# ScalarE copies the three plain edge fields, GpSimd adds the second weight parts: a two-layer graph network on Trainium2

## The reference

```python
h = relu(layernorm(x))
x = x + segment_sum((h @ W0)[src] * edge_weight[:, None], dst)
h = relu(layernorm(x)) @ W1.T + b1            # einsum('nd,od->no')
deg = 1 + count of edges with row == n        # self loops added
x = x + segment_sum(deg[row]**-.5 * deg[col]**-.5 * h[col], row)
```

## Time and profile before

| what | value |
|---|---|
| three runs | 1748.29, 1748.61, 1752.34 us |
| profiled execution, own time | 1750.08 us |
| its span | 1748.3 us |
| granted TensorE clock, mean of the span | 0.966 |
| busy PE / DVE / ACT / POOL, share of the span | 89% / 53% / 26% / 32% |

### The profile page before, as it was taken

One profiled execution on the slowest core, in us unless ns is written; L12 is line 12 of the kernel. 1 busy time (PEld: TensorE's weight loads), 2 busy tenths in 40 slices (PEclk: granted clock), 3 DMA queues, 4 the chain that ended last, 5 costly groups with the idle time before them and its releaser, 6 DMA issues.

```text
span 1748.3 us, 30157 instructions
## 1 busy us (share of the span) xinstructions
PE 1554.0 (89%) x8627; PEld 792.7 (45%) x8628; DVE 930.2 (53%) x1747; ACT 456.5 (26%) x783; POOL 556.2 (32%) x1494
## 2 busy tenths in 40 slices
PE   2566699995979999999998999979999999999998
PEld 1233355543545454444554545334444444444443
DVE  6956556425977678777776776382313131313121
ACT  2514454531212222222222222271212121212110
POOL 0112444213656677677676774000000000000000
PEclk9977899997989999999999999999999999999999
DMA  7201242107546565666565666671232323232310
GB/s 262 97 1 32 64 139 61 29 16 165 114 97 141 125 142 135 144 145 139 133 151 129 146 140 150 201 230 55 63 99 66 96 66 96 66 96 66 96 37 25
DMA packets 449659, 185.86 MB, mean 106 GB/s; under 512 B 376677, under 2 KB 431993, under 8 KB 449544
## 3 DMA queue, kind: packets, MB, share of 16 engines
q1 hardware_dynamic: 449544, 184.63, 41.5%
HBM read 77.06 MB, written 77.11 MB: 88 GB/s over the span
## 4 chain that ended last, share of the span: by engine, by line
PE 54%; DVE 14%; issue 11%; POOLq 5%; POOL 5%; DMA 4%; SPq 4%; DVEq 2%; ACT 2%; ACTq 0%
PE pair L1392 19%; PE pair L1304 12%; PE pair L1253 9%; PE pair L1316 7%; PE pair L1265 5%; POOLq L522 3%; POOL fbuf L525 2%; SPq L357 2%; POOL fbuf L527 2%; DVE slots L774 2%; DMA a_scratch<-area 2%; DVE slots L775 2%; DVE h L939 1%; PE pair L1422 1%; SPq L378 1%
## 5 line engine op out<-in xcount | busy, mean ns | idle before, releaser
L1316 PE MATMUL pair<-h,area 128*128 128x512 f16 x2400 | 551.0, 383 | 2.6 <-issue 1.9
L1316 PEld LDWEIGHTS pair<-h,area 128*128 128x128 f16 x2400 | 234.2, 99 | 265.5 <-issue 18.2
L1265 PE MATMUL pair<-slots 128*128 128x240 f16 x1624 | 209.3, 275 | 104.8 <-DVE slots L775 54.6
L525 POOL CAST fbuf<-etab 128x12 f16 (+1 forms) x640 | 192.9, 301 | 152.4 <-DVE slots L775 79.2
L1048 ACT ACTIVATE area<-pair 128x320 f32<-128x320 f32 x160 | 69.9, 437 | 643.2 <-PE pair L1265 439.9
L1265 PEld LDWEIGHTS pair<-slots 128*128 128x128 f16 x1624 | 157.3, 100 | 171.4 <-issue 73.0
L979 DVE SCALAR_TENSOR_TENSOR agg_s<-pair,sc,agg_s 128x512 f16<-128x512 f32 x40 | 28.2, 747 | 350.7 <-ACT agg_s L1172 350.7
L1304 PE MATMUL pair<-wmat,agg_t 128*128 128x512 f16 x960 | 210.4, 379 | 1.6 <-ACT agg_t L1179 1.6
L527 POOL TENSOR_TENSOR fbuf<-etab,negbase 128x4 f16 (+2 forms) x640 | 200.9, 314 | 0.0
L1392 PE MATMUL pair<-h,etab 128*128 128x512 f16 x800 | 182.1, 379 | 8.9 <-DVE h L939 8.7
L1392 PE MATMUL pair<-h,slots 128*128 128x512 f16 x800 | 180.5, 379 | 0.0
(11 more groups left out here) (181 smaller groups left out, 1316.1 us busy)
## 6 DMA issues: line engine op xcount, KB each, us to landing
c_scratch<-area SPq DMA_DIRECT2D x160, 160.0 KB, 2.2
a_scratch<-area SPq DMA_DIRECT2D x320, 80.0 KB, 2.2
area<-c_scratch SPq DMA_DIRECT2D x20, 1280.0 KB, 7.3
xt<-in_x SPq DMA_DIRECT2D x19, 512.0 KB, 3.6
x_scratch<-xt SPq DMA_DIRECT2D x19, 512.0 KB, 2.9
xt<-x_scratch SPq DMA_DIRECT2D x19, 512.0 KB, 3.6
out_x<-xt SPq DMA_DIRECT2D x19, 512.0 KB, 2.6
h<-x_scratch SPq DMA_DIRECT2D x4, 2048.0 KB, 10.5
```

The lines of the kernel that those rows point to most:

```text
L525: pool.tensor_copy(fbuf[:, s, 1:F, at].rearrange("p f u d -> p u f d"), twice(etab_c[:, bass.ds(c, u), 1:F], [P, u, F - 1, 2])).then_inc(s ...
L1265: return pe.matmul(dest, touches[:, t, 0:P], touches[:, t, P:CS], start=first, stop=last, skip_group_check=True)
L1316: last = pe.matmul(sum_pair(e)[:, half * H:(half + 1) * H], wts(e)[:, q, k, :], hpart(k, r)[:, half * H:(half + 1) * H], start=k == q == r ...
```

## The change

It has four parts.

- The copy of the three plain fields leaves GpSimd and becomes a ScalarE activation (`ACT.Copy`), in a `fields` of ScalarE's own, with its own load of the chunk number. GpSimd keeps the load and the addition of the key. There are 640 copies in all, four per quad.
- ScalarE issues the copies for quad n+2 just ahead of `window_out(n)`. They wait for the one-hots that read the same half of `fbuf` before.
- The addition of the weights' second parts, L823, leaves VectorE. `sum_counts` on GpSimd now waits for `win_evac` (VectorE's L820) in place of `win_act` (ScalarE's L1050), does this addition first and signals `win_lo`, on which the stores wait, and then adds to the degrees. There are 160 such additions.
- One-hots wait on two semaphores, `step_keys` and `step_fields`. The last tile is taken out of ScalarE's loop, since the last two quads have no later fields.

```diff
@@ GpSimd
-                    pool.tensor_copy(fbuf[:, s, 1:F, at].rearrange("p f u d -> p u f d"),
-                                     twice(etab_c[:, bass.ds(c, u), 1:F], [P, u, F - 1, 2])).then_inc(step_fields, 1)
                     pool.tensor_tensor(fbuf[:, s, 0, at], twice(etab_c[:, bass.ds(c, u), 0], [P, u, 2]),
-                                       twice(negbase[:, bass.ds(v0 + w, 1)], [P, u, 2]), ALU.add).then_inc(step_fields, 1)
+                                       twice(negbase[:, bass.ds(v0 + w, 1)], [P, u, 2]), ALU.add).then_inc(step_keys, 1)
...
             def sum_counts(n, s):
-                pool.wait_ge(win_act, n + 1)
+                pool.wait_ge(win_evac, n + 1)
+                pool.tensor_tensor(a_stage(s)[:, 1], a_stage(s)[:, 1], a_stage(s)[:, 2], ALU.add).then_inc(win_lo, 1)
@@ VectorE
-                dve.wait_ge(step_fields, 2 * UP_STEPS(n))
+                dve.wait_ge(step_keys, UP_STEPS(n))
+                dve.wait_ge(step_fields, UP_STEPS(n))
...
-                dve.wait_ge(win_evac, n + 1)
-                nc.vector.tensor_tensor(a_stage(s)[:, 1], a_stage(s)[:, 1], a_stage(s)[:, 2], ALU.add).then_inc(win_lo, 1)
@@ ScalarE
+            def fields(n, s, v0, count, u):
+                need(act, hots_ready, n - 1)
+                for w in range(count):
+                    act.load(c_reg, wtab[0:1, bass.ds((v0 + w) * 4, 1)])
+                    c = act.snap(c_reg[0], min_val=0, max_val=NCH)
+                    act.activation(fbuf[:, s, 1:F, w * u:(w + 1) * u].rearrange("p f u d -> p u f d"),
+                                   twice(etab_c[:, bass.ds(c, u), 1:F], [P, u, F - 1, 2]),
+                                   ACT.Copy).then_inc(step_fields, 1)
...
             def tile(td):
                 for q in range(QPT):
                     n = QPT * (td + PRE) + q
+                    if isinstance(n, int) and n < UQ:
+                        fields_of(2 * n + 2, 0)
+                        fields_of(2 * n + 3, 1)
+                    elif not isinstance(n, int) or n + 2 < NQ:
+                        fields_of(n + UQ + 2, q % 2)
                     window_out(n, q % 2, 2 * n + 2 if isinstance(n, int) and n < UQ else n + UQ + 1)
```

More of the change, by code:

```diff
@@ L225, in gnn_two_layers @@
         sup_free = sem("sup_free")
+        step_keys = sem("step_keys")
         step_fields = sem("step_fields")
@@ L1050, in window_out, with fields_of @@
                 act.activation(a_stage(s)[:, 2], sums[:, :, 2 * SB:3 * SB], ACT.Copy, scale=A_DOWN).then_inc(win_act, 1)
+            c_reg = [act.alloc_register("act_chunk")]
+            def fields(n, s, v0, count, u):
[6 more added lines that the diff above has]
+                                   ACT.Copy).then_inc(step_fields, 1)
+            def fields_of(n, s):
+                if isinstance(n, int) and n < 2 * UQ:
+                    fields(n, s, 2 * n, 2, UP)
+                else:
+                    fields(n, s, 4 * n - 4 * UQ, 4, UL)
             def STORED(n, s):
@@ L1121, in _ @@
                     act.wait_ge(table_ready, 1)
+                    act.wait_ge(etab_ready, F)
+                    fields_of(0, 0)
+                    fields_of(1, 1)
                 if t == min(W1_AT):
@@ L1129, in _ @@
                         std({1: 3, 6: 4, 9: 5}[w])
+                    fields_of(2 * w + 2, 0)
+                    fields_of(2 * w + 3, 1)
                     window_out(w, w % 2, 2 * w + 2, True)
@@ L1134, in _ @@
                 tile(td)
-            with act.Fori(UQ // QPT - PRE, T - PRE) as td:
+            with act.Fori(UQ // QPT - PRE, T - PRE - 1) as td:
                 tile(td)
+            tile(T - PRE - 1)
             def counts_first(e, done):
```

## The result

The changed kernel takes 1778.31 us (median, 1774.99 to 1779.54); the kernel before took 1748.45 us on the same chip (1747.96 to 1752.34). The ratio is 1.016, 95% interval 1.014 to 1.018. The change costs 29.9 us; the prediction had 11.8 for it, so it had the sign and not the size.

What follows compares the result with a forecast made beforehand. TensorE was taken to bound 447 to 1090 us, idling 50 us there. Nine pairs (+9.4 us) and quads 16 to 31 (+2.4) summed to +11.8 us, so 1760 us as a median, range 1738 to 1790.

Steps and rivals of the forecast that it cites:

- the term of -0.56 us for VectorE's branch back: In tiles with VectorE's branch back, it starts earlier by L823, -0.56 us, taking most of the 0.74 us wait.
- VectorE, per quad: Without L823 one-hots are ready 0.52 us sooner; one GpSimd addition of 320 elements costs them 0.67 us.
- the chain with L823 at both ends: From the last quad's L823 via stores, transposes and the next tile's L823 to TensorE's late step: 19 us.
- The term of +0.75 us for a tile without the branch back: Late step behind the transposes comes later: +0.2 us at the chain's start, +0.55 us at its end.
- ScalarE's copies at no cost: 640 ScalarE copies at 0.53 us each, 2.1 us a quad; lateness hidden by TensorE's dense products, cost none.
- GpSimd: right: GpSimd's quad: four key steps of 0.53 us and two additions of 0.90, 3.9 us against TensorE's 4.06; it just fits.
- The collision's 0.67 us: On VectorE's one-hots, one GpSimd addition of 320 elements running among them delays them by 0.67 us.
- The first tile of a pair: The tile with VectorE's branch back: earlier branch, longer addition and later chain end together give +0.3 us.
- "Quads 16 to 31", +2.4 us: Quads with two steps each and little VectorE room: each saves 0.52 and pays 0.67 us, 16 x 0.15.
- The count, nine pairs: 18 tiles (quads 16 to 159) make 9 pairs, each 1.05 us slower: +9.4 us.
- The rival with VectorE's relief: VectorE's relief from L823 outweighs collisions, making the kernel faster: 1739 us, or 1726 if one-hots never pay; chance 0.22.
- GpSimd and ScalarE as the bound: Two rivals, 1785 us each: GpSimd at 4.5 us a quad, chance 0.10; ScalarE's copies late, chance 0.08.

## Why the prediction was right or wrong

Three steps of the prediction failed: the term of -0.56 us for VectorE's branch back, which measured +1.52 us; the term "VectorE, per quad", which counted one collision where two occur; and a term that is missing, what a longer wait does to TensorE's clock, which is half of the loss (14.2 of 25 us).

*What bounds the kernel, and the chain with L823 at both ends: right.* The late steps stayed at the places of the earlier trace rows. The term of +0.75 us for a tile without the branch back measured +0.87, and about +1.0 with the loop written out.

*ScalarE's copies at no cost: right in the step between them, wrong at the branch back.* They stand 0.52 to 0.53 us apart, as read from GpSimd's step. Alone they cost 0.3%, and nothing once both loops are written out. But "VectorE takes it up only after the one-hots of quad n+1, later than that" does not hold for the last quad ahead of the branch back: the subtraction waits for `window_out` there. Writing ScalarE's loop out gave the changed kernel 10 us back, and nothing to the kernel before with VectorE's loop written out. That the copies in ScalarE's loop make the difference fits this, but the two were not compared with all else the same.

*GpSimd: right.* The addition took 0.854 us for 0.86; the key step rose with it, to 0.401 us, and GpSimd did not become the bound. The collision's 0.67 us was met to a hundredth: 1.35 for 0.68, 1.34 for 0.68. The prediction took the Trainium skill's rule of the exclusive lock (SBUF — State Buffer, "SBUF: two separate sides") to mean that the loser waits for all of the other's time, 0.86 us. The trace agrees with the rule and not with this reading of it: the loser comes when the other is already under way and is held until its end. A 1024 wide comparison ended 0.56 us behind the addition's end in one case and 0.55 in the other, out of its 0.68.

*"VectorE, per quad", -0.52 and +0.67: one hit too few.* In the quads that catch up both additions strike, 1.27 and 1.14 us for 0.68 and 0.48, +1.25 us. In the mean over all quads VectorE lost 0.53 of the 0.56 us it had been relieved of, so it gained next to no room with which a late quad is made good.

*The branch back, -0.56 us: wrong in sign.* "VectorE starts the branch back earlier by L823" failed, since ScalarE's lateness takes this up, and it supposed that the idle time behind it is fixed. That grew from 3.4 to 4.9 us in the mean. The first tile of a pair lost 0.98 us instead of 0.3. What lengthens it is not settled. It grows in each run that has the addition on GpSimd, also at a quarter of its length, and in no other. These runs have two things in common. One is that the stores start later against the branch: SP's pair of A stores beside it took 2.12 us to issue (at 802.43), 0.99 before (at 794.24). The other is that VectorE's own program is shorter, and the DMA view of each idle time shows a difference in the loading of instructions. Before the change, 793.52 to 796.69 us, and after it, 800.84 to 806.12 (number of loads, MB, share of the DMA engines' time):

```profile
q14 instruction: 1, 0.01, 1.1%
```

```profile
q14 instruction: 2, 0.02, 1.5%
```

It is one load in each of the seven idle times in the three runs that have the addition on VectorE and its loop as a loop (3.1 to 4.2 us), and two or more in each of the seven in the five runs that have it on GpSimd (4.4 to 6.3 us). So where the loop's ends fall in the code is a rival to the stores. The view does not say for which engine a load is. No run changed the one without the other; some empty instructions in VectorE's loop would.

*"Quads 16 to 31", +2.4 us: not there.* TensorE's idle time from 447 to 540 us went from 13.4 to 12.3 us.

*The count, nine pairs: seven.* The longer waits in the loop are 7 x 1.84 = 12.9 us, where the sum had 9 x 1.05 = 9.4. With small gains ahead of the loop they came out as 10.8 us of idle time. That this is near the 11.8 of the sum is errors that cancel.

*Missing altogether: the granted clock.* The sum priced a wait at its own length. Waits before the change stood mostly at 2.0 us and below, where the clock holds in all but a few cases. The change moved about one a pair beyond (3 of 22 were over 2.3 us before, 11 of 22 after), and each quad at the lower clock costs some 1.9 us more (20.7 / 11). This is half of the loss, 14.2 of 25 us. The rows for it were there: three quads of 5.7 to 6.8 us in the trace of before, behind waits of 2.0 to 3.3 us. The prediction read one chain, at 818.40 us, and that is a long wait that happened to have no such quad behind it.

The rival with VectorE's relief fell on the addition's 0.85 us; GpSimd and ScalarE as the bound did not come, though the time is near what these had.

## What to carry to other kernels

Work of two operands in SBUF that went from VectorE to GpSimd was hardly taken off VectorE: here 526 of 562 ns came back as blocked instructions, some of them on the steps everyone waits for. Look also at who waits for the engine that takes the work over: four small copies on ScalarE were cheap, and yet they made VectorE late at the quad ahead of its branch back. Price a longer wait of TensorE with the slower quad behind it: look in the trace of before whether its waits stand just short of the length at which this begins, since a few tenths then cost microseconds. And a loop's branch back on an engine that feeds the bound is a candidate of its own: writing one loop out won more (2%) than the change lost.

## What the runs showed of the hardware

- A wait of TensorE of 2 us or more was followed by a quad of over 5.3 us, part of it at the lower clock, in 86 of 104 cases; one of 0.6 to 2 us in 5 of 155. The edge is not sharp: once 3.46 us had no effect, and once 1.36 us had. The quad behind took 5.4 to 6.9 us instead of 4.06, mostly 5.7 to 6.0, and the next one 4.06.
- A VectorE comparison of 1024 float16 elements with both operands in SBUF takes 0.68 us alone and 1.34 to 1.35 beside a GpSimd addition of 320 elements. The subtraction that reads PSUM took 0.49 us beside one (at 849.00), as alone.
- An addition of 320 elements with both operands in SBUF takes GpSimd 0.79 us in float16 and 0.86 in float32, undisturbed. 80 elements take 0.37 us in the mean.
- ScalarE's register load with an activation of 12 elements a partition repeats every 0.53 us, of which 0.21 are the activation.
- A branch back of VectorE left it idle for 3.1 to 6.3 us, by the run: 3.1 to 4.2 with one load of instructions in the idle time, 4.4 to 6.3 with two or more. With the loop written out no idle time over 2 us before a first one-hot was left from 540 us on.
